# Value weights of a slot-attention decoder layer: one product for two sequences, and transfers that copy its parts to both partition halves

## The chip, the cores and the metric

One core of one Trainium2 chip runs the whole layer. TensorE (PE) multiplies, VectorE (DVE), ScalarE (ACT) and GpSimd (POOL) do the rest, and SyncE (SP) issues nearly all DMA transfers. The metric is the device time in microseconds (us); lower is better.

## The reference, cut to what matters

Four sequences of 1024 tokens, 256 wide, go through three sublayers. The change lies in the weights of the second one, in the `update` product.

```python
# 1: gated convolution and scan
proj = x @ W_in.T; g = sigmoid(gate); v = conv5(val) + conv_b
y[t] = tanh(a_param) * y[t-1] + g[t] * v[t]
x = layernorm(x + (layernorm(x + y @ W_out.T) * ln_w + ln_b))
# 2: every token is a slot; 64 context rows per sequence are the memory
Pn = rmsnorm(ctx); k = Pn @ Wk.T; v = Pn @ Wv.T
for _ in range(3):
    q = rmsnorm(slots) @ Wq.T
    attn = softmax(q @ k.T / 16, axis=slots); attn /= sum(attn over context) + eps
    updates = attn @ v                       # [1024, 256]
    slots = gru_cell(updates, slots, gru_wih, gru_whh, ...)
x = layernorm(x + slots)
# 3: each token goes to the expert with the highest score
x = layernorm(x + (x + x @ expert_w[argmax(x @ gate_w.T)]))
```

## The kernel before

The chip's work falls into three stretches that follow one another with some overlap.

**The first stretch** (about 0 to 168 us) is the convolution sublayer of the four sequences b = 0 to 3, as a software pipeline whose order is written out by hand for each engine in its own block; the engines meet by counting semaphores. For a sequence, PE projects (`project`, line 1138) into PSUM banks 0 to 3, ACT moves the values out and applies the sigmoid (`values(b, c)`, lines 538 to 549), DVE does the convolution taps and the scan (1625, 1643), PE multiplies by W_out (`output`, 1153), DVE adds and takes statistics (`residual`, 1654 to 1662), ACT normalises (`first_rows`, 568), DVE scales (`second`, 1696 to 1706), ACT normalises again (`second_rows`, 574), and PE transposes into PSUM (`transposes`, 1174), from where ACT writes the slots (`new_slots`, 637 and 638, `low_slots`, 645). Between them, ACT's `window` computes the square roots of one or two normalisations at once, and DVE's `offsets` (1673 to 1681) follows it. `transposes(0)` uses banks 6, 7, 0 and 1, the last two being banks of the gates, so it waits until ACT has read all gates of all sequences:

```python
pe.wait_ge(gate_ev, J * C * B)
pe.wait_ge(fold_ev, C)
pe.wait_ge(vp_lo, B)
```

**The second stretch** (about 168 to 430 us) is the three slot iterations, 6 half-iterations of 8 units, line 1452. Products there are made from a rounded high part and a low part of each operand. `at` holds the high part of the attention in one half of the 128 partitions and its low part in the other, 64 context rows each. So the value weights that meet it, v @ W_ih.T (`v_ih_pair`, 64 context rows, 768 columns), must stand in both halves, for each sequence, as a high part (w = 0) and a low part (w = 1).

**The third stretch** is the routing to the experts.

**The value weights** are made inside the first stretch. ACT writes the projected context twice side by side (`v_sb`, line 609), so that one product of PE yields 128 rows, the same 64 twice. For a sequence and a half of the columns (384, number i = 0 to 7) there are four steps: `value_input(i)` on PE (1225), `value_high(i)` on ACT rounds the product into `v_ih_pair` (620), `value_rest(i)` on PE subtracts the rounded part with `neg` (1232), `value_low(i)` on ACT writes what is left (626). Numbers 0 to 3 are done while sequences 2 and 3 are projected, numbers 4 to 7 after the last projection, ahead of `first_scores`, the scores of the first attention (PE 1255), which DVE's `first_tops` (1722) reads.

**The queue of SP** is in program order: the loads of the inputs (`load_fm`, 425 and 426, feature-major, and `load_tm`, 433 and 435, token-major), then the `save` transfers of the slots (441). `load_tm(3)` writes over the last part of `early_hi` and therefore waits until PE has projected all four sequences.

## Time and profile before

| What | Value |
|---|---|
| Median of 3 runs | 557.29 us (555.04 to 557.83) |
| Profiled execution, its own time | 557.2 us |
| Its span in the trace | 555.4 us |
| PE busy | 507.8 us, 91% |
| DVE busy | 438.9 us, 79% |
| ACT busy | 343.8 us, 62% |
| POOL busy | 250.5 us, 45% |
| Mean granted TensorE clock, share of full | 0.972 |

The span runs from the first to the last instruction in the trace; the profiled execution's time is 1.8 us longer. A busy share is an average over three stretches with different limits, so it does not say which engine sets the end of a stretch. Times inside the trace are counted from the start of the span.

### The profile page before, as it was taken

How to read it: one execution, taken by the hardware profiler on the slowest of the kernel's cores; microseconds unless marked ns; L12 is line 12 of the kernel's file. 1: busy time of each engine (PE TensorE's matmuls, PEld its weight loads, DVE VectorE, ACT ScalarE, POOL GpSimd, SP SyncE). 2: the span in 40 equal slices, each digit the busy share in tenths (PEclk: the TensorE clock that was granted, in tenths of full speed). 3: DMA queues.
4: the chain of work that ended last, by engine and by line, in shares of the span. 5: the costliest groups of instructions: out<-in, count | busy, mean ns of one | idle time of the engine just before them, and what ended most of it. 6: DMA issues, size and time to landing. Idle time of an engine off the chain costs nothing.

```text
span 555.4 us, 7269 instructions
## 1 busy us (share of the span) xinstructions
PE 507.8 (91%) x2174; PEld 366.0 (66%) x2174; DVE 438.9 (79%) x794; ACT 343.8 (62%) x608; POOL 250.5 (45%) x217
## 2 busy tenths in 40 slices
PE   6999986978779999899999999999997999979992
PEld 2465552845557687488768867885885788767771
DVE  2899999997799477989967985897677567868783
ACT  3657539786598474667466656765663766557453
POOL 0133050400223256556935664574335156737776
PEclk9999999899898999999999999999997999989997
DMA  8960202210021032000000000002111136255752
GB/s 299 316 194 2 76 1 76 76 44 33 0 77 63 15 77 77 0 2 0 2 1 1 0 0 1 2 1 76 40 38 39 38 128 235 91 159 157 222 153 71
DMA packets 28101, 39.98 MB, mean 72 GB/s; under 512 B 7421, under 2 KB 19838, under 8 KB 27776
## 3 DMA queue, kind: packets, MB, share of 16 engines
q1 hardware_dynamic: 24656, 31.10, 18.0%
q0 software_dynamic: 3408, 8.43, 4.1%
q8 instruction: 18, 0.29, 0.2%
q14 instruction: 19, 0.16, 0.1%
HBM read 25.70 MB, written 16.83 MB: 77 GB/s over the span
## 4 chain that ended last, share of the span: by engine, by line
PE 51%; DVE 6%; issue 6%; POOL 4%; ACT 3%; DMA 1%; SPq 0%; POOLq 0%; ACTq 0%; DVEq 0%
PE psum L1452 35%; PE psum L1542 7%; PE psum L1255 3%; PE psum L1394 2%; PE psum L1513 2%; PE psum L1340 1%; POOL gru L1005 1%; DVE gru L1865 1%; POOL sorted_rows L1035 1%; DVE slots_full L1867 1%; POOL out L1043 1%; POOL slots_lo L1020 1%; PE psum L1352 1%; DVE gru L1845 1%; PE psum L1416 1%
## 5 line engine op out<-in xcount | busy, mean ns | idle before, releaser
L1452 PE MATMUL psum<-slots_hi,w_hh 128*128 128x512 f32 x560 | 181.5, 406 | 1.2 <-ACT gru L752 1.2
L1452 PEld LDWEIGHTS psum<-slots_hi,w_hh 128*128 128x128 f32 x560 | 104.5, 191 | 27.8 <-issue 4.2
L1005 POOL TENSOR_TENSOR gru<-slots_full,gru 128x512 f32<-128x512 f32 x43 | 65.7, 1529 | 111.8 <-ACT gru L758 111.8
L1452 PE MATMUL psum<-slots_lo,w_hh 128*128 128x512 f32 x280 | 112.0, 400 | 0.0
L1452 PE MATMUL psum<-at,v_ih_pair 128*128 128x512 f32 x288 | 91.4, 402 | 5.0 <-DVE at L1744 3.1
L758 ACT ACTIVATE gru<-gru,vec 128x512 f32<-128x512 f32 x48 | 34.7, 722 | 58.7 <-DVE gru L1845 58.6
L1452 PEld LDWEIGHTS psum<-at,v_ih_pair 128*128 128x128 f32 x288 | 53.7, 190 | 21.9 <-DVE at L1744 3.4
L1838 DVE SCALAR_TENSOR_TENSOR gru<-psum,vec,gru 128x512 f32<-128x512 f32 x48 | 35.9, 747 | 36.0 <-PE psum L1452 30.2
L1138 PE MATMUL psum<-early_hi,w_in 128*128 128x512 f32 x128 | 57.9, 611 | 5.3 <-DMA early_hi<-in_xT 5.2
L1452 PEld LDWEIGHTS psum<-slots_lo,w_hh 128*128 128x128 f32 x280 | 53.4, 191 | 12.9
L1865 DVE TENSOR_TENSOR gru<-gru 128x512 f32<-128x512 f32 x47 | 43.7, 929 | 7.2 <-POOL gru L1005 3.7
L1138 PEld LDWEIGHTS psum<-early_hi,w_in 128*128 128x128 f32 x128 | 24.9, 196 | 36.0 <-issue 34.4
L1020 POOL TENSOR_TENSOR slots_lo<-slots_full,slots_hi 128x512 fp32r<-128x512 f32 x32 | 47.1, 1472 | 0.6 <-DVE slots_hi L1891 0.6
L752 ACT ACTIVATE gru<-psum,brz 128x512 f32<-128x512 f32 x48 | 32.7, 681 | 21.7 <-PE psum L1452 21.7
L1867 DVE TENSOR_TENSOR slots_full<-gru 128x512 f32<-128x512 f32 x47 | 44.5, 946 | 1.6
L1542 PE MATMUL psum<-slots_full,w_tile 128*128 x156 | 43.6, 403 | 0.4 <-issue 0.3
L1043 POOL DMA_INDIRECT out<-out_tile,out_index x39 | 38.0, 974 | 12.3 <-issue 6.1
L1035 POOL DMA_INDIRECT sorted_rows<-row_block,dest x32 | 33.8, 1056 | 19.9 <-DVE dest L1953 8.6
L1014 POOL TENSOR_TENSOR ss_block<-sq_block 128x512 f32<-128x512 f32 x16 | 22.3, 1393 | 40.6 <-ACT sq_block L773 37.0
L1845 DVE TENSOR_TENSOR gru<-psum,gru 128x512 f32<-128x512 f32 x48 | 33.2, 691 | 6.7 <-PE psum L1452 5.1
L765 ACT ACTIVATE gru<-psum,brz 128x512 f32<-128x512 f32 x48 | 32.5, 678 | 1.1 <-PE psum L1452 0.8
L1153 PE MATMUL psum<-w_out,gates 128*128 128x256 f32 x128 | 29.6, 386 | 2.6 <-DVE res L1654 2.3
(249 smaller groups left out, 878.3 us busy)
## 6 DMA issues: line engine op xcount, KB each, us to landing
gathered<-sorted_rows SPq DMA_DIRECT2D x39, 129.0 KB, 2.5
x_scratch<-slots_full SPq DMA_DIRECT2D x8, 512.0 KB, 3.0
x_block<-x_scratch SPq DMA_DIRECT2D x8, 512.0 KB, 4.1
early_hi<-in_xT SPq DMA_DIRECT2D x3, 1024.0 KB, 5.4
x_tm<-in_x SPq DMA_DIRECT2D x4, 512.0 KB, 6.3
slots_full<-expert_plus SPq DMA_DIRECT2D x1, 2048.0 KB, 10.3
sorted_rows<-gru SPq DMA_DIRECT2D x1, 1032.0 KB, 11.7
early_hi<-in_xT SPq DMA_DIRECT2D x2, 512.0 KB, 4.6
```

Of the source, the lines that this page charges most:

```text
L758: act.activation(X(u), X(u), ACT.Tanh, bias=col(c, V_BIH + 2)).then_inc(n_act, 1)
L1005: pool.tensor_tensor(DF(u), full[:, c, seq(k, h), blk(j)], X(u), ALU.subtract).then_inc(d_pool, 1)
L1020: last = pool.tensor_tensor(slots[1][:, c, b, blk(j)], full[:, c, b, blk(j)], slots[0][:, c, b, blk(j)].bitcast(F32), ALU.subtract)
L1035: pool.indirect_dma_start(rows[:], bass.IndirectOffsetOnAxis(dest[:, n:n + 1], 0), rowb[:, row_slot(n), :], None, bounds_check=E * REGION - 1,
L1043: pool.indirect_dma_start(out[:], bass.IndirectOffsetOnAxis(oidx[:, g % 4, t:t + 1], 0), og[:, i % (4 * TG), :], None, bounds_check=TOK - ...
L1138: last = pe.matmul(psum[:, bank + j, :], wi[:, k, at_col:at_col + P], xF[b % 2][:, k, cols_of(j)], start=k == 0, stop=k == C - 1)
L1452: last = pe.matmul(psum[:, bank, :], w, d, start=start and i == 0, stop=stop and i == len(pairs) - 1, skip_group_check=begun or late)
L1542: last = pe.matmul(expert_out(i), wT[:, i % TG, c, :], ew[:, c, bass.ds(off, D)], start=c == 0, stop=c == C - 1)
L1838: dve.scalar_tensor_tensor(out=X(u), in0=psum[:, hn_bank(u), :], scalar=col(c, V_BHH + 2), in1=X(u), op0=ALU.add, op1=ALU.mult).then_inc(t ...
L1845: dve.tensor_tensor(X(u), psum[:, XN_B, :], X(u), ALU.add).then_inc(t2_dve, 1)
L1865: dve.tensor_tensor(Z(u), Z(u), DF(u), ALU.mult).then_inc(e_dve, 1)
L1867: dve.tensor_tensor(full[:, c, seq(k, h), blk(j)], X(u), Z(u), ALU.add).then_inc(s_dve, 1)
```

## The change

A product now takes the context rows of two sequences (`pair` 0 is sequences 0 and 1): rows 0 to 63 are the one's value weights, rows 64 to 127 the other's. So there are four products instead of eight, i = 0 to 3, and i // 2 is the pair. `v_sb` holds each row once. ACT writes the high and low parts of a product no longer into `v_ih_pair` but into three buffers `value_part0` to `value_part2`, used in turn: the parts are numbered n = 0 to 7, four to a pair (high, high, low, low), and part n goes to buffer n % 3. `spread_value(pair)` on SP's queue waits for each part and issues four transfers of 64 partitions x 384 columns (98,304 bytes) from the buffer to `v_ih_pair`: for each of the two sequences one to the lower and one to the upper half. They count on three semaphores `vp_out`, one for each buffer. ACT waits on these before it writes a buffer again (`free_part`), and PE before the first products that read `v_ih_pair`. `spread_value(0)` stands after `load_tm(2)`, `spread_value(1)` after `load_tm(3)`. The second group of steps, numbers 4 to 7, is gone on PE and ACT.

```diff
@@ SBUF and helpers @@
+        value_parts = [sb2(f"value_part{i}", [P, G3 // 2], F32R) for i in range(3)]
-        sb2("value_place", [P, 3 * C * B * M - P])
+        sb2("value_place", [P, 3 * C * B * M - P - 3 * G3 // 2])
-        v_sb = gru[:, 3:5, :].rearrange("p c (b h m) -> p c b h m", b=B, h=2)
+        v_sb = gru[:, 3:5, 0:B * M].rearrange("p c (b m) -> p c b m", b=B)
         def value_bank(i):
-            return TBS[i % 2] if i < B else VB + i % 2
+            return TBS[i % 2]
+        def high_part(i):
+            return 4 * (i // 2) + i % 2
@@ sync @@
+                def spread_value(pair):
+                    for n in range(4 * pair, 4 * pair + 4):
+                        w, h = n // 2 % 2, n % 2
+                        sp.wait_ge((vp_hi, vp_lo)[w], 2 * pair + h + 1)
+                        for b in range(2):
+                            for to in range(2):
+                                sp.dma_start(v_ih[pair][half(to), b, w, h * HG:(h + 1) * HG].bitcast(F32),
+                                             value_parts[n % 3][half(b), :].bitcast(F32)).then_inc(vp_out[n % 3], 16)
                 load_tm(2)
+                spread_value(0)
                 load_tm(3)
+                spread_value(1)
                 for b in range(B):
                     save(b)
@@ scalar @@
-                        twice = psum[:, OB + c, 0:BM].rearrange("p (b h m) -> p b h m", b=B, h=1).broadcast_to(
-                            [P, B, 2, M])
-                        act.activation(v_sb[:, c], twice, ACT.Copy).then_inc(v_ev, 1)
+                        act.activation(v_sb[:, c].rearrange("p b m -> p (b m)"), psum[:, OB + c, 0:BM],
+                                       ACT.Copy).then_inc(v_ev, 1)
+                def free_part(n):
+                    if n > 2:
+                        act.wait_ge(vp_out[n % 3], 64 * (n // 3))
                 def value_high(i):
                     act.wait_ge(vp_mm, i + 1)
-                    act.activation(vp(0, b)[:, h * HG:(h + 1) * HG], psum[:, value_bank(i), 0:HG],
+                    free_part(high_part(i))
+                    act.activation(value_parts[high_part(i) % 3][:], psum[:, value_bank(i), 0:HG],
                                    ACT.Copy).then_inc(vp_hi, 1)
                 def value_low(i):
                     act.wait_ge(vp_sub, i + 1)
-                    act.activation(vp(1, b)[:, h * HG:(h + 1) * HG], psum[:, value_bank(i), 0:HG],
+                    free_part(high_part(i) + 2)
+                    act.activation(value_parts[(high_part(i) + 2) % 3][:], psum[:, value_bank(i), 0:HG],
                                    ACT.Copy).then_inc(vp_lo, 1)
                 window(3)
-                value_high(4)
-                value_high(5)
                 first_rows(2)
-                value_low(4)
-                value_low(5)
                 new_slots(1)
                 spread_roots(0, OB)
                 low_slots(1)
-                value_high(6)
-                value_high(7)
                 window(4)
-                value_low(6)
-                value_low(7)
@@ tensor @@
-                    if i == B:
-                        pe.wait_ge(val_ev, J * C * B)
-                    if i % B >= 2:
+                    if i >= 2:
                         pe.wait_ge(vp_lo, i - 1)
@@ first_hidden @@
-                        pe.wait_ge(vp_lo, 2 * B - 1 + q)
+                        pe.wait_ge(val_ev, J * C * B)
@@ unit @@
+                    if q == 0 and k < 2:
+                        for i, done in enumerate(vp_out):
+                            pe.wait_ge(done, 64 * len(range(i, 4 * k + 4, 3)))
```

Three places show how this moves the instructions. First ACT, from the second normalisation of sequence 1 to the transposed slots of sequence 0. Before:

```order
L582 ACTIVATE rrs<-rrs 128x8 [waits rr_act]
L620 ACTIVATE v_ih_pair0<-psum 128x384 [waits vp_mm] x2
L538 ACTIVATE early_lo<-psum 128x512 [waits val_mm,conv]
L538 ACTIVATE early_lo<-psum 128x512 [waits val_mm]
L543 ACTIVATE slots_full<-early_lo,vec 128x1024 [waits scanned,val_ev]
L549 ACT_TABLE_LOAD [waits gate_mm]
L549 ACTIVATE gates<-psum 128x512 [waits out_mm]
L549 ACTIVATE gates<-psum 128x512 [waits gate_mm]
L626 ACTIVATE v_ih_pair0<-psum 128x384 [waits vp_sub] x2
L574 ACTIVATE res<-res,nms,rss 128x256 [waits off2]
L574 ACTIVATE res<-res,nms,rss 128x256 x7
```

And with the change (its line numbers are those of the changed file):

```order
L599 ACTIVATE rrs<-rrs 128x8 [waits rr_act]
L640 ACTIVATE value_part1<-psum 128x384 [waits vp_out_1,vp_mm]
L640 ACTIVATE value_part2<-psum 128x384 [waits vp_out_2,vp_mm]
L555 ACTIVATE early_lo<-psum 128x512 [waits val_mm,conv]
L555 ACTIVATE early_lo<-psum 128x512 [waits val_mm]
L560 ACTIVATE slots_full<-early_lo,vec 128x1024 [waits scanned,val_ev]
L566 ACT_TABLE_LOAD [waits gate_mm]
L566 ACTIVATE gates<-psum 128x512 [waits out_mm]
L566 ACTIVATE gates<-psum 128x512 [waits gate_mm]
L646 ACTIVATE value_part0<-psum 128x384 [waits vp_out_0,vp_sub]
L646 ACTIVATE value_part1<-psum 128x384 [waits vp_out_1,vp_sub]
L591 ACTIVATE res<-res,nms,rss 128x256 [waits off2]
```

The order is the same, but each of the four writes of parts now waits for transfers too, and `second_rows(0)` stands behind the last of them, `value_low(3)`, which is part 7 in buffer 1.

Next SP's queue from `load_tm(2)` on. Before:

```order
L435 DMA x_tm<-in_x 128x4x256 [waits add_done]
L435 DMA x_tm<-in_x 128x4x256
L435 DMA early_hi<-in_x 128x4x256 [waits gate_mm,val_mm]
L435 DMA early_hi<-in_x 128x4x256
L441 DMA x_scratch<-slots_full 256x1x512 [waits x1_ev] x8
```

With the change, from `load_tm(3)` on (the four parts of pair 0, in the same form, stand between `load_tm(2)` and these rows):

```order
L440 DMA early_hi<-in_x 128x4x256 [waits gate_mm,val_mm]
L440 DMA early_hi<-in_x 128x4x256
L449 DMA v_ih_pair<-value_part 64x384 [waits vp_hi]
L449 DMA v_ih_pair<-value_part 64x384 x3
L449 DMA v_ih_pair<-value_part 64x384 [waits vp_hi]
L449 DMA v_ih_pair<-value_part 64x384 x3
L449 DMA v_ih_pair<-value_part 64x384 [waits vp_lo]
L449 DMA v_ih_pair<-value_part 64x384 x3
L449 DMA v_ih_pair<-value_part 64x384 [waits vp_lo]
L449 DMA v_ih_pair<-value_part 64x384 x3
L456 DMA x_scratch<-slots_full 256x1x512 [waits x1_ev] x8
```

The transfers of part 4, the first of pair 1, now stand behind `load_tm(3)` and its wait for the last projection.

Last PE, between the transposes of sequence 1 and the first scores. Before:

```order
L1174 MATMUL psum<-ident,res 128x128
L1225 MATMUL psum<-gru 128x384 [waits val_ev]
L1225 MATMUL psum<-gru 128x384 x3
L1232 MATMUL psum<-v_ih_pair,neg 128x384 [waits vp_hi] x2
L1245 MATMUL psum<-ident,rrs 64x128 [waits res_done,rr_act]
L1245 MATMUL psum<-ident,rrs 64x128 x15
L1225 MATMUL psum<-gru 128x384 [waits vp_lo]
L1225 MATMUL psum<-gru 128x384
L1225 MATMUL psum<-gru 128x384 [waits vp_lo]
L1225 MATMUL psum<-gru 128x384
L1183 MATMUL psum<-slots_hi,neg 128x512 [waits x1_hi] x4
L1255 MATMUL psum<-slots_full,fold 64x512 [waits rstd_done,x1_low,x1_ev,fold_ev]
```

With the change:

```order
L1186 MATMUL psum<-ident,res 128x128
L1255 MATMUL psum<-ident,rrs 64x128 [waits res_done,rr_act]
L1255 MATMUL psum<-ident,rrs 64x128 x15
L1195 MATMUL psum<-slots_hi,neg 128x512 [waits x1_hi] x4
L1265 MATMUL psum<-slots_full,fold 64x512 [waits rstd_done,x1_low,x1_ev,fold_ev]
```

Eight products and their four subtractions are gone from this place and its surroundings; the second stretch has the same instructions in the same order as before.

## Rows read from the trace of the kernel before

**Rows 1.** Page, engines: busy us, share of the span, instructions.

```profile
PE 507.8 (91%) x2174; PEld 366.0 (66%) x2174; DVE 438.9 (79%) x794; ACT 343.8 (62%) x608; POOL 250.5 (45%) x217
```

**Rows 2.** The chain that ended last, from its first piece on: start, us, what.

```profile
156.88 2.16 DVE res L1699
...
233.25 15.09 PE psum L1452 x64
```

**Rows 3.** Timeline of DVE, 102 to 132 us: start, busy, idle and releaser in brackets.

```profile
102.88 0.16 DVE L1677 SCALAR_TENSOR_TENSOR nms<-mvs,rss 128x8 f32<-128x8 f32 x1
...
105.41 0.68 DVE L1654 TENSOR_TENSOR res<-psum,x_tm 128x512 f32<-128x512 f32 x1
...
109.96 0.69 DVE L1654 TENSOR_TENSOR res<-psum,x_tm 128x512 f32<-128x512 f32 x1 [0.25 <-PE psum L1153]
...
113.21 0.16 DVE L1673 SCALAR_TENSOR_TENSOR nms<-mvs,rss 128x8 f32<-128x8 f32 x1
...
128.44 0.17 DVE L1681 TENSOR_TENSOR rrs<-rrs,rss 128x8 f32<-128x8 f32 x1
129.91 1.23 DVE L1722 CUSTOM_DVE_ANT_0 sc<-psum,inv 128x1024 f32<-128x1024 f32 x1 [1.31 <-PE psum L1255]
```

**Rows 4.** Timeline of ACT, 65 to 78 us.

```profile
66.32 0.49 ACT L626 ACTIVATE v_ih_pair<-psum 128x384 fp32r<-128x384 f32 x1 [0.15 <-PE psum L1232]
...
77.25 0.31 ACT L561 ACTIVATE rss<-mvs,epsc 128x16 f32<-128x16 f32 x1 [9.14 <-DVE mvs L1662]
```

**Rows 5.** Timeline of ACT, 89 to 127 us.

```profile
89.01 0.88 ACT L626 ACTIVATE v_ih_pair<-psum 128x384 fp32r<-128x384 f32 x2
89.75 4.04 ACT L574 ACTIVATE res<-res,nms,rss 128x256 f32<-128x256 f32 x8
...
98.65 0.21 ACT L563 ACTIVATE rss<-rss 128x8 f32<-128x8 f32 x1
...
115.42 4.03 ACT L568 ACTIVATE res<-res,nms,rss 128x256 f32<-128x256 f32 x8
119.35 0.84 ACT L626 ACTIVATE v_ih_pair<-psum 128x384 fp32r<-128x384 f32 x2
120.09 0.58 ACT L637 ACTIVATE slots_full<-psum 128x512 f32<-128x512 f32 x1
...
123.92 1.08 ACT L653 ACTIVATE inv<-psum 128x1024 f32<-128x1024 f32 x1
124.82 2.12 ACT L645 ACTIVATE slots_lo<-psum 128x512 fp32r<-128x512 f32 x4
```

**Rows 6.** Timeline of PE, 85 to 135 us.

```profile
85.11 7.28 PE L1138 MATMUL psum<-early_hi,w_in 128*128 128x512 f32 x16
97.06 3.68 PE L1174 MATMUL psum<-ident,res 128*128 128x128 f32 x16 [4.66 <-ACT gates L549]
100.53 4.05 PE L1153 MATMUL psum<-w_out,gates 128*128 128x256 f32 x16
104.22 1.28 PE L1183 MATMUL psum<-slots_hi,neg 128*128 128x512 f32 x4
106.23 3.69 PE L1153 MATMUL psum<-w_out,gates 128*128 128x256 f32 x16 [0.73 <-DVE res L1654]
...
126.11 3.65 PE L1255 MATMUL psum<-slots_full,fold 128*64 128x512 f32 x16 [1.49 <-ACT slots_lo L645]
```

**Rows 7.** Timeline of SP: `load_tm(3)`.

```profile
92.47 0.92 SPq L435 DMA_DIRECT2D early_hi<-in_x  x2
```

**Rows 8.** Page, DMA issues: count, KB each, us to landing.

```profile
gathered<-sorted_rows SPq DMA_DIRECT2D x39, 129.0 KB, 2.5
```

**Rows 9.** DMA between 91 and 100 us: issues, us to landing.

```profile
early_hi<-in_x SPq DMA_DIRECT2D x2, 512.0 KB, 4.1
```

**Rows 10.** Windows: stretch, length, busy of each engine, clock, DMA share, GB/s.

```profile
95.00:96.00 1.00, 0.00 (x0) 0.00 (x0) 0.97 (x2) 1.00 (x2) 0.00 (x0) 0.50 1.08 381
...
101.00:102.00 1.00, 1.00 (x5) 0.86 (x4) 0.90 (x2) 1.00 (x3) 0.00 (x0) 0.81 0.37 141
```

More of the change, by code:

```diff
@@ L158, in decoder_layer @@
         vp_mm, vp_hi, vp_sub, vp_lo = sem("vp_mm"), sem("vp_hi"), sem("vp_sub"), sem("vp_lo")
+        vp_out = [sem(f"vp_out_{i}") for i in range(3)]
         wh_hi, wh_lo = sem("wh_hi"), sem("wh_lo")
@@ L615, in folded @@
                                        scale=col(c, V_SN)).then_inc(fold_ev, 1)
+                def free_part(n):
+                    if n > 2:
+                        act.wait_ge(vp_out[n % 3], 64 * (n // 3))
                 def value_high(i):
-                    b, h = i // 2, i % 2
                     act.wait_ge(vp_mm, i + 1)
-                    act.activation(vp(0, b)[:, h * HG:(h + 1) * HG], psum[:, value_bank(i), 0:HG],
+                    free_part(high_part(i))
+                    act.activation(value_parts[high_part(i) % 3][:], psum[:, value_bank(i), 0:HG],
                                    ACT.Copy).then_inc(vp_hi, 1)
                 def value_low(i):
-                    b, h = i // 2, i % 2
                     act.wait_ge(vp_sub, i + 1)
-                    act.activation(vp(1, b)[:, h * HG:(h + 1) * HG], psum[:, value_bank(i), 0:HG],
+                    free_part(high_part(i) + 2)
+                    act.activation(value_parts[(high_part(i) + 2) % 3][:], psum[:, value_bank(i), 0:HG],
                                    ACT.Copy).then_inc(vp_lo, 1)
@@ L1213, in value_input @@
                 def value_input(i):
-                    b, h = i // 2, i % 2
+                    pair, h = i // 2, i % 2
                     if i == 0:
@@ L1219, in value_input @@
                         pe.wait_ge(neg_set, 1)
-                    if i == B:
-                        pe.wait_ge(val_ev, J * C * B)
-                    if i % B >= 2:
+                    if i >= 2:
                         pe.wait_ge(vp_lo, i - 1)
                     for k in range(C):
-                        last = pe.matmul(psum[:, value_bank(i), 0:HG], v_sb[:, k, b].rearrange("p h m -> p (h m)"),
+                        last = pe.matmul(psum[:, value_bank(i), 0:HG],
+                                         v_sb[:, k, 2 * pair:2 * pair + 2].rearrange("p b m -> p (b m)"),
                                          wih_r[:, k, h * HG:(h + 1) * HG], start=k == 0, stop=k == C - 1)
@@ L1229, in value_rest @@
                 def value_rest(i):
-                    b, h = i // 2, i % 2
                     pe.wait_ge(vp_hi, i + 1)
-                    pe.matmul(psum[:, value_bank(i), 0:HG], neg[:], vp(0, b)[:, h * HG:(h + 1) * HG],
+                    pe.matmul(psum[:, value_bank(i), 0:HG], neg[:], value_parts[high_part(i) % 3][:],
                               start=False, stop=True, skip_group_check=True).then_inc(vp_sub, 1)
@@ L1313, in _ @@
                 transposes(1)
-                value_input(4)
-                value_input(5)
-                value_rest(4)
-                value_rest(5)
                 spread(0, OB)
-                value_input(6)
-                value_input(7)
                 low_parts(1)
                 first_scores(0, S_B)
-                value_rest(6)
-                value_rest(7)
                 for q in range(2):
```

## The prediction

> **What bounds the kernel now.** I read three views: the busy shares, the chain that ended last, and the timelines of the engines around the changed steps. PE is busy for 91% of the span and DVE for 79% [rows 1], and from about 230 us on the chain runs through PE's products almost alone [rows 2]. That stretch has the same instructions before and after, so it can only start earlier or later, not become shorter. The chain's first piece is at 156.88 us on DVE [rows 2]; before that the profile gives no chain, and I follow the timelines. From 105.41 us DVE adds the residual of sequence 2 and goes on nearly without a gap, with 0.25 us of idle at 109.96 [rows 3], until it has finished the offsets at 128.44 + 0.17 = 128.61 us and waits 1.31 us for the first scores of PE [rows 3]. So DVE sets the pace of this stretch, with 1.31 us to be had at its end. PE is not the bound here: it sits idle 4.66 us before the transposes at 97.06, released by ACT's gates, 0.73 us before 106.23 and 1.49 us before the scores [rows 6].
>
> **What the change removes.** Eight evictions on ACT between 113 and 131 us go: two of them take 0.84 us at 119.35 [rows 5], so all eight about 3.4 us. Eight products' worth of work goes from PE there. None of this is DVE's work. It pays only where DVE waits for it, which is the 1.31 us before the scores. The copy of the context (`v_sb`) is half as wide, a few tenths of a microsecond in front of ACT work that DVE does not wait for; I cost it at nothing. Pair 1 is now made by the steps that before made sequence 1: the same count at the same place. With everything else unchanged the gain would be 1.3 us.
>
> **What it adds: the first wait.** `value_low(1)` writes part 3 into the buffer of part 0, and must wait for part 0's four transfers. Before, it starts at 66.32 us, and afterwards ACT is idle for 9.14 us until 77.25 [rows 4]. SP takes 0.92 / 2 = 0.46 us to issue a transfer [rows 7], and a small one of 129 KB lands 2.5 us after its issue [rows 8]. Even if SP began only at 66.32, the four would be there at 66.32 + 4 x 0.46 + 2.5 = 70.7 us. The idle stretch hides this 4.3 us; with that cover gone it would be paid in full. PE has nothing queued behind it that is needed before 77 us, except the next value products.
>
> **The second wait.** `value_low(3)` writes part 7 into buffer 1, from which part 4 must have been sent. Part 4's transfers are on SP's queue behind `load_tm(3)`. SP issues that load only when the last projection is over, from 92.47 to 92.47 + 0.92 = 93.39 us [rows 7], while ACT comes to `value_low(3)` at 89.01 + 0.88 / 2 = 89.4 us [rows 5]. The wait is certain; its length is the main term. The projection itself is not held up: it ends at 85.11 + 7.28 = 92.39 us [rows 6] and needs of ACT only the gates that stand ahead of the parts.
>
> - Low end: SP issues the last of four transfers at 93.39 + 3 x 0.46 = 94.8; landing 2.5 us later [rows 8] gives 97.3.
> - The two loads ahead of them move 2 x 512 KB and land 4.1 us after their issues [rows 9], the second at about 92.93 + 4.1 = 97.0. The four parts are 393 KB and stand behind these. At the 381 GB/s of the window at 95 us [rows 10] they need 1.0 us more, so 98.0, and at half that rate, should half the partitions mean half the rate, 99.1.
>
> No row shows a copy between partitions or one of 64 partitions. I take 98.5, between the queue's two rates, since the queue is full when the parts enter it. ACT's wait is then 98.5 - 89.4 = **9.1 us** (7.9 to 9.7).
>
> A rule speaks against these transfers: the Trainium skill, "SBUF — State Buffer", section "Door 1: The DMA port swizzle", says that partitions 0 to 63 reach only 8 of 16 ports, and that a transfer over them gets about half the bandwidth of one over 128; the section on two DMAs adds that two such transfers at once do not make up for it. By that rule the release would be at 99.1 and the forecast 0.6 us later; by the window's rate alone it would be 98.0 and 0.5 us earlier. Every load shown here has 128 partitions, so no run here shows it yet.
>
> **Who waits behind it.** Behind `value_low(3)` on ACT stand `second_rows(0)` (89.75), the values and gates of sequence 3's second half, `window(2)` (ending 98.65 + 0.21 = 98.86) [rows 5] and the slots of sequence 0. All shift by 9.1. PE's transposes wait for these gates: 97.06 becomes 106.2. DVE's offsets at 102.88 [rows 3] wait for `window(2)`, now at 108.0. On PE everything follows: transposes, the first half of `output(2)`, the low parts, ending 104.22 + 1.28 = 105.50 before [rows 6]. There PE waited 0.73 us for DVE; now it does not. So the second half of `output(2)`, and DVE's last residual at 109.96, which waits for it, come 9.1 - 0.73 = **8.4 us** later. DVE's slack at its first residual is used up, since 105.41 lies far before 100.53 + about 2 + 9.1. From there on DVE is busy without a gap as before, so it reaches 128.61 + 8.4 = 137.0 us.
>
> Are the scores ready by then? The offset at 113.21 + 0.16 = 113.37 [rows 3] becomes 121.8. `first_rows(2)` before had started 2 us after its offset, at 115.42, behind removed evictions; now it starts at 121.8 and takes 4.03. The slots take 123.92 - 120.09 = 3.83, the spreading 0.90, and half of the four low parts 1.06 [rows 5]: 131.6. The scores take 3.65 [rows 6]: 135.3. That is 1.7 us before 137.0, so the 1.31 us of idle is gone: 8.4 - 1.3 = **7.1 us**.
>
> **The clock.** PE's granted clock had fallen to 0.50, 1.2 GHz, in the window at 95 us, after its last product had ended at 92.39, and is 0.81 in the window from 101 to 102, some 4 us after work began again at 97.06 [rows 6, 10]. The longer idle stretch now costs the same half-clock stretch once, just later. But PE will also be idle, by my count of its shifted rows, from about 122, where products were removed, to 126.3 (121.8 + 4.03 + 0.5), when the first slots of sequence 1 come, and may run the scores slowly. At half clock throughout they would end at 131.6 + 7.3 = 138.9 and DVE would wait 1.9 us. Between 0 and 1.9 I take 0.3, because the four products of low parts come first and by the time of the scores most of the return to 2.4 GHz has passed.
>
> **Sum.** Waiting 9.1, less 0.73 of PE's wait, less 1.31 of DVE's wait, plus 0.3 of clock: 7.4 us. The profiled execution took 557.2 us for a span of 555.4, and the median is 557.29, the same to 0.1. The forecast is 557.2 + 7.4 = **564.6 us**, 1.3% slower. The transfers add 32 issues, 3.1 MB in all, on SP; the saves behind them wait for the slots of their sequence anyway, and what is saved is read only in the last iterations.
>
> **The rivals.**
> - *The clock costs more.* With the removed products PE has more gaps: to the one at 122 comes one of about 2 us between the first hidden products and `output(3)`, on which DVE waits. If the clock falls there too, half clock for some 4 us adds about 2 us, and with the scores' 1.9: 566.5 to 568.5. The long idle stretch at 92 us speaks for it, against it speaks that 2 us is short beside the 4.66 us of idle around which the clock had fallen [rows 6].
> - *ACT's wait is not on the path, and the change is not slower.* The chain of shifts breaks even at a wait of 0.73 + 1.31 = 2.0 us, and stays within 0.5% (2.8 us) up to 4.8. That needs part 4 to land by 94.2, 0.8 us after the load's issue, or a queue of SP that does not hold the parts back. With no wait the 1.31 us is the whole change: 555.9 us. Against it: 93.39 + 1.84 us of issuing alone is past 94.2.
> - *Half of the loss is given back by ACT.* If DVE were not the bound between 112 and 128, the shift would be ACT's: 8.4 less the 2.06 between 113.36 and 115.42 and less 0.74 of the evictions at 119.35 [rows 5], that is 5.6, and 562.8 us. Against it: DVE's gapless timeline.
> - *The first wait is longer than 9.14 us too*, through slow transfers between partitions. Then the second is longer as well, by as much, and the time is over 570 us.
>
> **How the numbers follow.** The forecast's mechanism, with waits of 7.9 to 9.7 us, has 0.66 and gives 563.1 to 565.5. More clock cost has 0.15 (to 568.5), ACT giving back 0.07 (562.8), much slower transfers 0.04, and the hidden wait 0.08. The range 561.5 to 568.0 leaves out the last two and a little of the clock's case. One measurement of this kernel tells about 0.5%, 2.8 us, from no change. Faster by more than that needs a gain that no row offers: 0.02, out of the hidden wait's 0.08. Within it: the other 0.06. Slower: 0.92.
>
> **What would show it in the changed profile.** ACT's second L646 write of the pair-1 low parts should start near 98.5, with some 9 us of idle released by a transfer; the first stall, near 66 us, should be under 4.3 us and leave the square roots at 77 us in place. PE's transposes should start near 106.2 and DVE's first scores reduction near 137, with no idle before it. The slot iterations should keep their length. The prediction is wrong if the parts land before the load that was issued ahead of them, if DVE has slack that I took for work, or if the stretch after 168 us changes its length.

## The result

The changed kernel took 564.16 us in the median of 4 runs (563.31 to 564.88), the kernel before 556.69 us (4 runs). The ratio is 1.0136, with a 95% interval of 1.0105 to 1.0167: slower by 7.5 us. Forecast were 564.6 us, a shift of 7.4 from 557.2, and a range of 561.5 to 568.0.

The page of the changed kernel gives the span and the busy shares that answer to [rows 1]:

```profile
span 563.1 us, 7262 instructions
...
PE 501.4 (89%) x2154; PEld 359.7 (64%) x2154; DVE 438.1 (78%) x794; ACT 339.9 (60%) x600; POOL 251.4 (45%) x217
```

PE works 6.4 us less and ACT 3.9 us less than before, and the span is 7.7 us longer. What was removed is gone, and the time is not in any engine's work. So it is in a wait. The timeline of ACT around the parts of pair 0 and pair 1 shows both waits (start, busy, form, and in brackets the idle time ahead and its releaser):

```profile
69.56 0.49 ACT L646 ACTIVATE value_part<-psum 128x384 fp32r<-128x384 f32 x1 [2.49 <-DMA v_ih_pair<-value_part]
...
78.48 0.31 ACT L578 ACTIVATE rss<-mvs,epsc 128x16 f32<-128x16 f32 x1 [7.13 <-DVE mvs L1667]
...
90.23 0.50 ACT L646 ACTIVATE value_part<-psum 128x384 fp32r<-128x384 f32 x1
100.40 0.49 ACT L646 ACTIVATE value_part<-psum 128x384 fp32r<-128x384 f32 x1 [9.67 <-DMA v_ih_pair<-value_part]
100.78 4.03 ACT L591 ACTIVATE res<-res,nms,rss 128x256 f32<-128x256 f32 x8
```

The first wait is 2.49 us and lies inside the idle stretch that was there before: 7.13 us are still left of it at 78.48, where [rows 4] had 9.14. The second has 9.67 us in its bracket, released by a transfer into `v_ih_pair`; counted as the forecast counts it, from where part 7 could have started, half an eviction pair (0.4 us) after 90.23, it is 9.8 us. Behind it the work of ACT starts at 100.78, where [rows 5] had 89.75. SP's timeline shows why part 4's transfers came so late:

```profile
65.43 10.20 SPq L449 DMA_DIRECT2D v_ih_pair<-value_part  x16
93.69 0.92 SPq L440 DMA_DIRECT2D early_hi<-in_x  x2
94.65 10.15 SPq L449 DMA_DIRECT2D v_ih_pair<-value_part  x16
```

The load goes out at 93.69, and then 16 transfers in a row, about 0.6 us each. The profiled execution also began 1.2 us later than that of before: ACT reaches its square roots at 78.48, where [rows 4] had 77.25, and DVE stood 1.2 us behind already at 61 us, before the first part. It comes from the stretch in which the inputs are loaded and projected, which the change doesn't touch: at 9 us the two executions are within 0.1 us of each other (8.90, and 9.01 before), and then ACT's next eviction of the input's projection starts at 11.79 instead of 10.88. So 1.2 us must be taken off each start below. PE's timeline answers to [rows 6]:

```profile
86.33 7.28 PE L1150 MATMUL psum<-early_hi,w_in 128*128 128x512 f32 x16
108.07 3.68 PE L1186 MATMUL psum<-ident,res 128*128 128x128 f32 x16 [14.46 <-ACT gates L566]
...
122.51 1.97 PE L1255 MATMUL psum<-ident,rrs 128*64 128x128 f32 x32
128.76 0.80 PE L1195 MATMUL psum<-slots_hi,neg 128*128 128x512 f32 x1 [4.29 <-ACT slots_hi L658]
...
133.63 5.22 PE L1265 MATMUL psum<-slots_full,fold 128*64 128x512 f32 x16 [1.19 <-ACT slots_lo L665]
```

And DVE's timeline answers to [rows 3]:

```profile
109.90 0.17 DVE L1682 SCALAR_TENSOR_TENSOR nms<-mvs,rss 128x8 f32<-128x8 f32 x1 [5.71 <-ACT rss L580]
...
114.26 0.69 DVE L1659 TENSOR_TENSOR res<-psum,x_tm 128x512 f32<-128x512 f32 x1 [3.92 <-PE psum L1165]
...
118.54 0.69 DVE L1659 TENSOR_TENSOR res<-psum,x_tm 128x512 f32<-128x512 f32 x1 [1.17 <-PE psum L1165]
...
120.27 0.69 DVE L1659 TENSOR_TENSOR res<-psum,x_tm 128x512 f32<-128x512 f32 x1 [0.25 <-PE psum L1165]
...
138.56 0.17 DVE L1686 TENSOR_TENSOR rrs<-rrs,rss 128x8 f32<-128x8 f32 x1
139.01 1.22 DVE L1727 CUSTOM_DVE_ANT_0 sc<-psum,inv 128x1024 f32<-128x1024 f32 x1 [0.29 <-PE psum L1265]
```

PE's idle time ahead of the transposes is 14.46 instead of 4.66 us, and 4.29 us have appeared ahead of the low parts, after 122.51 + 1.97, where products were removed. DVE, which had gone from 97 to 128 us almost without a gap, stands still for 5.71, 3.92 and 1.17 us. (One operation of that stretch was itself a hidden wait: in the kernel before, the 128 x 8 product of line 1681, at 103.15, took 2.34 us, where it takes 0.17 at 110.18 here. Over the same time, from 103.10 for 2.36 us, POOL worked on a product of line 969; here POOL does that one at 104.34, while DVE is waiting anyway. That DVE was held up by POOL there, and with it PE for its 0.73 us, is what these rows suggest; no run tests it.) At the end of the stretch DVE waits 0.29 us for the first scores instead of 1.31, although these now take 5.22 us instead of 3.65. The windows say why (stretch, length, busy time of PE, its weight loads, DVE, ACT and POOL, granted clock, DMA share, GB/s):

```profile
98.00:99.00 1.00, 0.00 (x0) 0.00 (x0) 1.00 (x2) 0.00 (x0) 0.00 (x0) 0.50 1.09 326
99.00:100.00 1.00, 0.00 (x0) 0.00 (x0) 1.00 (x1) 0.00 (x0) 0.00 (x0) 0.50 1.07 274
126.00:130.00 4.00, 1.07 (x2) 0.57 (x2) 3.81 (x4) 4.00 (x9) 0.00 (x0) 0.57 0.00 0
130.00:134.00 4.00, 2.47 (x5) 0.90 (x7) 3.87 (x7) 4.00 (x9) 0.00 (x0) 0.50 0.70 262
134.00:138.00 4.00, 4.00 (x14) 1.26 (x12) 3.93 (x14) 0.97 (x3) 0.00 (x0) 0.65 0.00 0
```

PE's clock is 0.50, 1.2 GHz, from 130 to 134 us and 0.65 in the mean of the next 4, which hold the scores. The first two rows show the DMA engines fully busy while the copies of pair 1 follow the load; they are used further down.

### The profile page after: what moved, and what is told of

It reads as the page before. It is cut to its first block, busy times and chain, and to the rows that moved or that the text cites. A ratio compares the mean times of both kernels' runs of the same rounds, so it can differ in the third digit from the quotient of the medians.

```text
span 563.1 us, 7262 instructions
## 1 busy us (share of the span) xinstructions
PE 501.4 (89%) x2154; PEld 359.7 (64%) x2154; DVE 438.1 (78%) x794; ACT 339.9 (60%) x600; POOL 251.4 (45%) x217
## 4 chain that ended last, share of the span: by engine, by line
PE 50%; issue 6%; DVE 6%; POOL 4%; ACT 3%; DMA 1%; SPq 0%; POOLq 0%; ACTq 0%; DVEq 0%
PE psum L1454 35%; PE psum L1547 7%; PE psum L1265 3%; PE psum L1396 2%; PE psum L1518 2%; PE psum L1342 1%; POOL gru L1017 1%; DVE gru L1870 1%; POOL sorted_rows L1047 1%; DVE slots_full L1872 1%; POOL out L1055 1%; POOL slots_lo L1032 1%; PE psum L1354 1%; DVE gru L1850 1%; ACT gru L777 1%
```

## The experiments

Each kernel was timed with the kernel before beside it on the same chip; ratios are to that. Rows with the same time of before were measured together. The change itself, 564.16 us and 1.0136, stands above. In the code cuts `...` marks lines left out.

| Kernel | Median us | Before beside it | Ratio (95% interval) |
|---|---|---|---|
| Four buffers | 556.21 | 556.94 | 0.9989 (0.9974 to 1.0005) |
| Queue swapped | 556.11 | 556.94 | 0.9994 (0.9978 to 1.0010) |
| Two buffers | 565.78 | 556.94 | 1.0176 (1.0144 to 1.0207) |
| Before, with one wait | 564.09 | 556.94 | 1.0139 (1.0095 to 1.0183) |
| No transfers | 556.32 | 557.25 | 0.9978 (0.9964 to 0.9992) |
| Queue swapped, gap partly filled | 556.37 | 557.25 | 0.9986 (0.9973 to 0.9999) |
| Full width | 564.22 | 557.25 | 1.0121 (1.0100 to 1.0143) |
| Queue swapped, gap filled through | 554.40 | 557.15 | 0.9952 (0.9935 to 0.9969) |
| Queue swapped, again | 555.93 | 557.15 | 0.9980 (0.9964 to 0.9996) |

### Four buffers: the wait taken away, the transfers kept

Theory A is the prediction's: ACT's wait for transfers behind the load is the loss. Theory B says that the transfers themselves cost the time, theory C that the gaps left on PE lower its clock. The first experiment adds a fourth buffer, in a row of `gru` that is unused at that time, so that no part waits for one that stands behind the load. PE waits once for all parts.

```diff
-        vp_out = [sem(f"vp_out_{i}") for i in range(3)]
+        vp_out = [sem(f"vp_out_{i}") for i in range(4)]
...
+        value_parts.append(gru[:, 5, 0:G3 // 2].bitcast(F32R))
...
-                    if n > 2:
-                        act.wait_ge(vp_out[n % 3], 64 * (n // 3))
+                    if n > 3:
+                        act.wait_ge(vp_out[n % 4], 64 * (n // 4))
...
-                    if q == 0 and k < 2:
-                        for i, done in enumerate(vp_out):
-                            pe.wait_ge(done, 64 * len(range(i, 4 * k + 4, 3)))
+                    if q == 0 and k == 0:
+                        for done in vp_out:
+                            pe.wait_ge(done, 128)
```

> The change with a fourth part buffer (an unused row of gru), so that part 7 no longer waits for part 4; all 32 transfers stay, in the same place of SP's queue. Theory A (ACT's wait for transfers that stand behind load_tm(3) is the loss): the 9.8 us of idle on ACT at 90 us and the 2.5 us at 67 us are gone, PE's transposes start within 1 us of 97 us plus the run's own offset, and the time is that of the kernel before less DVE's 1.3 us of wait for the first scores: 555 to 557 us. Theory B (the transfers themselves, their 32 issues and 3.1 MB, cost the time): stays at 561 or more. Theory C (the products taken from PE leave gaps in which its clock falls): no wait, but 558 to 561.

It took 556.21 us, 0.9989 of before. With all 32 transfers in the same queue the loss is gone. ACT writes parts 6 and 7 without a wait, and DVE's first scores come at 130.35. There was one surprise, in the timelines of PE and DVE:

```profile
118.82 0.49 PE L1196 MATMUL psum<-slots_hi,neg 128*128 128x512 f32 x1 [4.14 <-ACT slots_hi L659]
...
123.70 6.49 PE L1266 MATMUL psum<-slots_full,fold 128*64 128x512 f32 x16 [1.19 <-ACT slots_lo L666]
```

```profile
130.35 1.22 DVE L1728 CUSTOM_DVE_ANT_0 sc<-psum,inv 128x1024 f32<-128x1024 f32 x1 [1.57 <-PE psum L1266]
```

PE has 4.14 us of idle ahead of the first product of the low parts, as in the changed kernel. The scores take 6.49 us, and DVE waits 1.57 us for them, more than the 1.31 of before. Theory A had the loss right, but the gain of 1.3 us that the removed products should have left is not there in this execution. Theory C is alive for this part, with the size of the gain and not of the loss.

### Queue swapped: the same by another way

```diff
                 load_tm(2)
                 spread_value(0)
-                load_tm(3)
                 spread_value(1)
+                load_tm(3)
```

> The change with two lines of SP's queue swapped: spread_value(1) ahead of load_tm(3). Three buffers and all transfers stay. Theory A: part 4 is sent from about 86 us and has landed when ACT comes to part 7 at 90.6 us, so ACT waits under 1 us; 555 to 557.5 us; the load of sequence 3 comes some 3 us later, 40 us before it is read. Theory B: 561 or more, as the same transfers run. Theory C: 558 to 561.

It took 556.11 us, 0.9994 of before, and 555.93 us, 0.9980, when it was measured again. SP issues the load at 94.74 instead of 92.47 (in the kernel before), and nobody waits for it. The first scores take 6.38 us and DVE waits 1.45 us. Two edits that have nothing in common but that part 7 no longer waits for the load give the same time.

### Two buffers: a longer wait

```diff
-        value_parts = [sb2(f"value_part{i}", [P, G3 // 2], F32R) for i in range(3)]
+        value_parts = [sb2(f"value_part{i}", [P, G3 // 2], F32R) for i in range(2)]
...
-                    if n > 2:
-                        act.wait_ge(vp_out[n % 3], 64 * (n // 3))
+                    if n > 1:
+                        act.wait_ge(vp_out[n % 2], 64 * (n // 2))
```

> The change with two part buffers instead of three: part 6 now waits for part 4 and part 7 for part 5, whose four issues of 0.6 us each follow behind. Theory A: ACT is released about 2.4 us later than with three buffers (at 102.8 instead of 100.4), and all of it shows: 564.2 + 2.4 = 566.6 us. Theories B and C: the same transfers and the same products, so 564.2 within 1 us.

It took 565.78 us, 1.6 us more than the change, where 2.4 were expected. The timeline of ACT has the reason:

```profile
78.00 0.31 ACT L578 ACTIVATE rss<-mvs,epsc 128x16 f32<-128x16 f32 x1 [4.12 <-DVE mvs L1667]
...
100.33 0.49 ACT L646 ACTIVATE value_part<-psum 128x384 fp32r<-128x384 f32 x1 [10.46 <-DMA v_ih_pair<-value_part]
101.56 0.49 ACT L646 ACTIVATE value_part<-psum 128x384 fp32r<-128x384 f32 x1 [0.73 <-DMA v_ih_pair<-value_part]
```

Parts 6 and 7 wait one behind the other, as was said, but part 5's transfers land 1.23 us after part 4's and not 2.4 us: they were issued while part 4's stood behind the load. ACT goes on at 101.56, which against the square roots at 78.00 is 23.56 us, and in the changed kernel 100.40 - 78.48 = 21.92. The wait grew by 1.6 us and the median by 1.6 us. The mechanism held, and the size of the step was expected wrong. The intervals of the two ratios overlap (1.0144 to 1.0207, and 1.0105 to 1.0167, four runs each), so the step is seen in the trace and only likely in the times. The kernel also says what the release hangs on: SP issues four copies in 2.4 us, and they landed 1.23 us behind the four before, so behind the load the pace was not that of SP's issues.

### Before, with one wait: the loss without the change

```diff
                 def value_low(i):
                     act.wait_ge(vp_sub, i + 1)
+                    if i == 3:
+                        act.wait_ge(xt_in[1], 16 * J * 2)
```

> The kernel before with one wait added and nothing else: value_low(3) on ACT waits until load_tm(3) has landed (about 97.0 us), 7.7 us after ACT comes to it. No part buffers, no copies, all eight products. Theory A: the 7.7 us less the 0.73 us that PE waited for DVE, with DVE's wait for the scores kept: +7.0, 563.7 us. Theory B: no transfers of parts, so little of the loss, under 559 us. Theory C: all products are there, under 559 us.

It took 564.09 us, 7.15 us more than before. The kernel has no buffers, no copies between partitions and all eight products, and one added wait reproduces the loss. ACT's timeline shows the wait for the load, and DVE's the first scores:

```profile
89.58 0.50 ACT L628 ACTIVATE v_ih_pair<-psum 128x384 fp32r<-128x384 f32 x1
98.10 0.49 ACT L628 ACTIVATE v_ih_pair<-psum 128x384 fp32r<-128x384 f32 x1 [8.02 <-DMA early_hi<-in_x]
```

```profile
139.13 1.23 DVE L1724 CUSTOM_DVE_ANT_0 sc<-psum,inv 128x1024 f32<-128x1024 f32 x1 [3.00 <-PE psum L1257]
```

The wait is 8.02 us. Less 0.73 it gives 7.3, near the 7.15. The nearness is worth little, since the four runs spread widely, from 561.1 to 567.4 (an interval of 5.3 to 10.2 us on the loss), and in the profiled one the scores came 3.00 us late for DVE, instead of 1.31, and took 5.35 us. PE's clock was 1.00 until 130 us, 0.98 from there to 134, and 0.60 in the mean from 134 to 138, although all eight products were in place; in the kernel before it was 1.00 over the same work. So the clock can fall here with the products there too.

### No transfers: what the copies themselves cost

ACT writes the parts straight into `v_ih_pair`, and PE uses the place of a pair's first sequence for both. The distribution to the halves of the partitions is left out.

```diff
-            return v_ih[b // 2][:, b % 2, w, :]
+            return v_ih[b // 2][:, 0, w, :]
...
-                spread_value(0)
...
-                spread_value(1)
...
-                    free_part(high_part(i))
-                    act.activation(value_parts[high_part(i) % 3][:], psum[:, value_bank(i), 0:HG],
+                    act.activation(vp(0, i // 2 * 2)[:, i % 2 * HG:(i % 2 + 1) * HG], psum[:, value_bank(i), 0:HG],
...
```

> The change without its 32 transfers and without the waits on them: ACT writes the four products' parts straight into v_ih_pair, and PE uses the first sequence's place for both of a pair (this leaves out the distribution to the halves). The products 4 to 7 are gone as in the change. Theory A (only the wait behind load_tm(3) cost time, the transfers themselves nothing): the same as with four buffers or with the swapped queue, 556.1 us within 1. Theory B (transfers also cost a little): 1 us or more below these, 555.0 or less. Theory C (the gap on PE lowers its clock): DVE still waits about 1.5 us for the first scores, and these take over 6 us instead of 3.65.

It took 556.32 us, 0.9978 of before (0.9964 to 0.9992), where the two kernels with all transfers and no late wait had 0.9989, 0.9994 and 0.9980. The intervals overlap: the 32 transfers cost less than can be told here, at most some tenths of a percent. The first scores take 6.50 us again and DVE waits 1.57 us, with no transfer in the kernel. So the slow scores have nothing to do with the copies.

### The gap partly filled

In the kernel with the swapped queue, five products whose result nobody reads go into PE's gap ahead of the low parts of sequence 1.

```diff
                 spread(0, OB)
+                for i in range(5):
+                    pe.matmul(psum[:, VB, 0:HG], v_sb[:, 0, 0:2].rearrange("p b m -> p (b m)"),
+                              wih_r[:, 0, 0:HG], start=True, stop=True)
                 low_parts(1)
```

> The kernel with the swapped queue, and five products on PE whose result nobody reads, in the 4.1 us gap ahead of low_parts(1), from which the change took products. Theory C (clock): PE's clock stays at 2.4 GHz, the scores take 3.65 instead of 6.4 us, DVE's 1.45 us of wait goes, and the time is 1.3 to 1.5 us lower than with the swapped queue alone: 554.6 to 554.8 against 556.1 us. If the clock is not what ate the gain: no difference, 556.1 us, and the scores stay at 6.4 us.

It took 556.37 us, 0.9986: no difference that can be told from the swapped queue alone. The windows show that the theory was not yet tested, first the swapped queue and then this kernel:

```profile
118.00:122.00 4.00, 2.77 (x4) 1.05 (x4) 3.88 (x7) 4.00 (x9) 0.00 (x0) 0.59 0.35 131
122.00:126.00 4.00, 2.82 (x7) 0.85 (x8) 3.84 (x15) 2.30 (x5) 0.00 (x0) 0.50 0.35 131
126.00:130.00 4.00, 4.00 (x13) 1.27 (x10) 2.52 (x5) 0.51 (x2) 0.00 (x0) 0.63 0.00 0
```

```profile
118.00:122.00 4.00, 1.87 (x6) 0.61 (x4) 3.88 (x8) 4.00 (x10) 0.00 (x0) 0.95 0.33 125
122.00:126.00 4.00, 2.82 (x7) 1.11 (x9) 3.84 (x8) 2.76 (x5) 0.00 (x0) 0.50 0.36 137
126.00:130.00 4.00, 4.00 (x13) 1.23 (x10) 3.05 (x13) 0.51 (x2) 0.00 (x0) 0.70 0.00 0
```

The mean clock from 118 to 122 us rose from 0.59 to 0.95, and then it fell to 0.50, 1.2 GHz, as before. The scores, from 123.93 on, still took 5.85 us. Ahead of the fall PE worked on the single products of the low parts, which come at ACT's pace, about 0.5 us of work and 0.47 us of idle time each, until the last of them took 0.80 us:

```profile
119.06 0.49 PE L1195 MATMUL psum<-slots_hi,neg 128*128 128x512 f32 x1 [0.73 <-ACT slots_hi L658]
...
121.95 0.80 PE L1195 MATMUL psum<-slots_hi,neg 128*128 128x512 f32 x1 [0.47 <-ACT slots_hi L658]
```

I had filled the gap ahead of them and not the ones between them.

### The gap filled through

Here `idle_products(n)` issues n of the products whose result nobody reads, as shown in the section above, and `low_parts` calls the function that it is given behind each of its four products.

```diff
                 spread(0, OB)
-                low_parts(1)
+                idle_products(6)
+                low_parts(1, lambda: idle_products(1))
+                idle_products(2)
                 first_scores(0, S_B)
...
```

> The swapped queue, and products whose result nobody reads filling PE from the spread of the roots to the first scores: six ahead of low_parts(1), one behind each of its four products, two ahead of the scores. The five of the run before only moved the fall of the clock from about 120 to 122 us. Theory C (the clock ate the gain): now the clock stays at 1.00 through 114 to 130 us, the scores take 3.65 to 3.9 us, DVE waits under 0.2 us for them, and the first scores of the slot iterations come 1.2 to 1.5 us earlier against the run's own start than with the swapped queue alone; 554.8 us, ratio to before 0.997. If another chain holds this stretch up, DVE's wait is shorter but what follows it waits longer, and the time is that of the swapped queue.

It took 554.40 us, 0.9952 of before (0.9935 to 0.9969). This kernel is 0.5% faster than the kernel before, and 10 us faster than the changed one. Its windows, and the scores on PE and DVE:

```profile
118.00:122.00 4.00, 3.92 (x14) 1.97 (x13) 3.88 (x7) 4.00 (x8) 0.00 (x0) 1.00 0.36 134
122.00:126.00 4.00, 4.00 (x18) 1.63 (x18) 3.84 (x15) 2.23 (x6) 0.00 (x0) 1.00 0.34 128
126.00:130.00 4.00, 4.00 (x20) 2.40 (x17) 3.93 (x8) 0.62 (x3) 0.00 (x0) 1.00 0.00 0
```

```profile
123.69 3.65 PE L1267 MATMUL psum<-slots_full,fold 128*64 128x512 f32 x16
```

```profile
128.33 1.23 DVE L1736 CUSTOM_DVE_ANT_0 sc<-psum,inv 128x1024 f32<-128x1024 f32 x1
```

The clock stays at 1.00, 2.4 GHz, the scores take 3.65 us, and DVE starts on them at 128.33 with no wait, 1.6 us before the 129.91 of [rows 3], where this execution's own start is the same to 0.1 us. At this place the gain that was to be had, 1.3 us, is now there.

> The swapped queue once more, for a comparison on the same chip: 0.999 of before, scores at half clock for 6.4 us, DVE waiting 1.45 us for them.

Beside it the swapped queue alone took 555.93 us, 0.9980 (0.9964 to 0.9996). The medians are 1.5 us apart as expected. The two were measured together, so their runs can be set against each other: eleven of the twelve of the filled kernel lie below the median of the other, and drawing again at random from the two sets gives a difference of 0.6 to 2.1 us (95%). The mean granted clock of a run was 0.974 to 0.984 with the filling and 0.963 to 0.976 without. What the traces do not show is the whole way from the scores to the end. The first scores of the slot iterations, counted from each run's square roots, come 0.8 and 0.3 us earlier than in the swapped queue's two traces (188.60 - 77.20 against 189.54 - 77.38 and 189.35 - 77.63), not the 1.2 to 1.5 us expected, and 0.7 us earlier than in the kernel before (189.36 - 77.25), where the medians are 2.7 us apart. The profiled execution itself took 555.86 us, more than the 555.03 of the swapped queue beside it. So that the filling keeps the clock up and makes the kernel faster is shown, and where all of the time is won stays open.

In the execution of the swapped queue that was profiled here, the scores took 5.03 us and DVE did not wait, against 6.38 us and 1.45 in the execution profiled before: when the clock comes back is different from run to run.

### Full width: is it the half of the partitions?

Each transfer moves the same bytes as 128 partitions x 192 columns. The kernel leaves out the placing of the parts: the bytes do not stand where the products look for them.

```diff
-                                sp.dma_start(v_ih[pair][half(to), b, w, h * HG:(h + 1) * HG].bitcast(F32),
-                                             value_parts[n % 3][half(b), :].bitcast(F32)).then_inc(vp_out[n % 3], 16)
+                                at_col = h * HG + to * HG // 2
+                                sp.dma_start(v_ih[pair][:, b, w, at_col:at_col + HG // 2].bitcast(F32),
+                                             value_parts[n % 3][:, to * HG // 2:(to + 1) * HG // 2].bitcast(F32)).then_inc(vp_out[n % 3], 16)
```

> The change with each transfer made over 128 partitions x 192 columns instead of 64 x 384, the same 98,304 bytes and the same number and place in the queue (the contents are put in wrong places). If transfers of half the partitions move at a lower rate, the queue behind the two loads drains faster, ACT is released about 1 us sooner after the load's issue (5.7 instead of 6.7 us) and the time falls by about 1 us, to 563.2. If the rate is set by the issues on SP, 0.6 us each, or by latency, the release stays at 6.7 us after the load's issue and the time at 564.2.

It took 564.22 us, the same as the change's 564.16. ACT is released 99.86 - 93.24 = 6.62 us after SP begins to issue the load, and in the changed kernel 100.40 - 93.69 = 6.71. Late in the stretch in which the DMA engines are fully busy, when little of the load can be left, the rates differ. In this kernel they moved 352 GB/s from 98 to 99 us, 4.8 to 5.8 us after SP began to issue the load:

```profile
98.00:99.00 1.00, 0.00 (x0) 0.00 (x0) 1.00 (x2) 0.00 (x0) 0.00 (x0) 0.50 1.11 352
```

In the changed kernel the same stretch is 98.5 to 99.5 us, between the two rows shown above, and the rate there is 292 GB/s. So the narrower copies ran at 0.83 of the rate, not at half, and only 0.1 us of it reaches ACT. Two things keep this from being a measurement of one copy. The copies of a part lie in both halves of the partitions in turn, and several are on their way at once. And the full-width ones are made of pieces half as long (768 bytes instead of 1,536), which may cost them something; no run separates the two.

The scores of this kernel matter for another reason. It waits like the changed kernel, and has the same products, but in its profiled execution, the slowest of its four at 566.39 us, PE's clock was 0.50 from 130 to 138 us, over most of the scores, and DVE waited for them:

```profile
132.60 6.66 PE L1266 MATMUL psum<-slots_full,fold 128*64 128x512 f32 x16 [1.18 <-ACT slots_lo L666]
```

```profile
139.41 1.23 DVE L1728 CUSTOM_DVE_ANT_0 sc<-psum,inv 128x1024 f32<-128x1024 f32 x1 [1.73 <-PE psum L1266]
```

## Why the prediction was right

**The mechanism.** Each link was seen: the wait at part 7, released by a transfer of part 4 behind the load; the transposes, the offsets and the residual of DVE shifted behind it. Taking the wait away by two ways removed the loss, a wait 1.6 us longer went with a median 1.6 us higher, and a wait alone, in the kernel before, cost 7.15 us (5.3 to 10.2).

**The terms.** ACT's wait was forecast at 9.1 (7.9 to 9.7) and is 9.8 us: mis-sized by 0.7, just past its upper bound. SP took 0.60 us for each of these copies, where I took the 0.46 of a load [rows 7], but the two-buffer kernel shows that the issues did not set the pace. The term that was mis-sized is the landing of the second load. The 4.1 us of [rows 9] is the median of the two, and I used it for the second as well. Asked one by one, in the trace of the kernel before, the first lands 3.6 us after its issue and the second 4.6: at 97.5 us and not at 97.0. The kernel with one wait shows it too, where ACT is released at 98.10, which is 4.6 us after 93.04 + 0.46. In the changed kernel they took 3.4 and 4.8 us, so the second landed at 94.15 + 4.8 = 98.9, or 97.7 without the later start. From there to the release at 99.2 it was 1.5 us, as forecast. Behind the load the copies landed up to 4.5 us after their issue; the median of all 32 is 2.2. PE's 0.73 us came off as said: DVE's last residual is at 120.27, which is 10.31 later than in [rows 3], 9.1 without the later start, and 9.8 - 0.73 = 9.1. The scores then begin on DVE 9.10 us later, 7.9 without the start, against 7.4 forecast.

**The clock.** I had given it 0.3 us at the scores, and DVE's wait there is 0.29 us. That is luck. The scores took 5.22 us at the mixed clock. In two other profiled executions with the late wait and the same products they took 6.66 us (full width) and 6.62 us (two buffers), and DVE waited 1.73 and 1.70 us, near the 1.9 us that the prediction gives for half clock throughout. So this term goes from 0.3 to 1.7 us in three traces, and the reason given for 0.3, that most of the return to 2.4 GHz has passed by the time of the scores, does not hold in general. The prediction's "with everything else unchanged the gain would be 1.3 us" left the clock out as well: without the late wait the scores took 5.0 to 6.5 us, and in four of these five traces DVE waited 0.92 to 1.57 us for them. In the medians the gain was 0.7 to 1.2 us, with no change inside or close to the edge of each interval; with the gaps filled it was 2.7. The estimate of 555.9 us for the hidden wait came out nearly (556.2, 556.1 and 555.9), since a change of that size is not far from none.

**What lies between 7.9 and the result.** The traces of the two kernels differ further on in ways that are not the change's: from the scores to the first scores of the slot iterations the shift grows by 1.1 us (on DVE 199.57 against 189.36), with PE's clock at half from 176 to 180 us, and in the routing it shrinks again, by 1.2 and 1.6 us, the second time with a different clock around the first expert tiles. The swapped queue's two executions differ in the same place, the clock 0.83 and 1.00 between 485 and 495 us, with spans of 555.2 and 553.2. The plain times say the same: of the twelve runs of the swapped queue's first measurement the five with a mean clock of 0.975 or 0.976 took 555.06 to 555.46 us, and the seven with 0.963 to 0.967 took 555.72 to 557.66. So a single trace of this kernel carries about 2 us of such differences either way, and that the sum met the median to 0.4 us is partly luck. The slot iterations themselves did not change: from one iteration's first scores to the next one's it is 51.6 us in both. The spread that the prediction gives its mechanism is a little wider than its sum: waits of 7.9 to 9.7 us, less 0.73 and 1.31 and plus 0.3, make 563.4 to 565.2 us, not 563.1 to 565.5.

**The rule on partitions.** The Trainium skill, "SBUF — State Buffer", section "Door 1: The DMA port swizzle", would have had half the bandwidth for 64 partitions. The trace agrees in direction only, 292 against 352 GB/s for copies that follow one another in both halves, and with the full-width kernel the release moved by 0.1 us, not by the 1 us expected of a halved rate. The forecast by it, 0.6 us more, was near the measured wait, but for another reason, the later landing of the second load.

**The rivals.** The hidden wait, the give-back by ACT and the first wait of over 9.14 us did not occur; the first wait was 2.49. More clock cost did not occur in the changed kernel's four runs (563.31 to 564.88). In the full-width kernel's profiled execution, at 566.39 us, DVE's wait of 1.73 us was just what this rival describes.

## What to carry to other kernels

A small ring of buffers that is emptied by transfers ties its writer to everything that stands ahead in the issuing queue, waits included. Ask of each reuse which queue must have passed which wait first; here two lines in the other order take 8 us away. Work taken from an engine that was waiting anyway gains only what others waited for, and on TensorE the clock can take part of that back: look at the granted clock of the stretch that follows the removed work, not only at its busy time.

## What I had not expected of the hardware

- PE's clock fell from 1.00 to 0.50 while the engine had work: in the partly filled kernel it was doing the single products of the low parts, one by one as ACT delivered them, 0.49 to 0.51 us each at first, with 0.47 us of idle time between. With products put into those gaps too it stayed at 1.00, 2.4 GHz, and the scores behind them took 3.65 instead of 5.85 us.
- The same kernel in two executions had its scores at 6.38 and at 5.03 us, and its routing at clocks of 0.83 and 1.00.
- SP took 0.60 us for each of a row of copies from SBUF to SBUF of 64 x 384, against 0.46 us for a load of 512 KB on a queue that had stood idle. It is not the kind of transfer alone: with the swapped queue the same two loads, right behind a row of copies, took 1.15 us, 0.58 each.
- Moving 32 of these copies, 3.1 MB, beside the work of all engines cost nothing that the times can show.
